# Layers 2 to 5 of a six-layer recurrent net: whole halves of the batch, weights stationary, gates turned in place of products

## The chip, the cores and the metric

One core of one Trainium2 chip. The metric is the device time of one execution in microseconds, as the median of several executions. TensorE (PE in the profile) multiplies, VectorE (DVE), ScalarE (ACT) and GpSimd (POOL) do the elementwise work, and transfers are issued from SyncE (SP), ACT and POOL. SBUF is the working memory, PSUM the memory that TensorE writes.

## The reference

```python
for i in range(6):                       # NLAYERS
    gate = ih[i][token]                  # (1024, 256), rows of a table of 4000
    state = jnp.tanh(state + jnp.matmul(state, hh[i]) * gate)
return state                             # (1024, 256) float32
```

Tokens run from 49 to 31985, the table has 4000 rows, and an index beyond its end takes the last row, number 3999. So about seven tokens in eight take that row.

## The kernel before, in words

The state is kept turned: 256 hidden units on partitions, as two blocks c = 0, 1 of 128, and the batch along the free dimension. The batch of 1024 is cut into four quarters of 256, each of two tiles of 128. A step n is a layer and a quarter (l, q = divmod(n, 4)); there are 24. All tensors of a step have 128 x 512 elements.

Layers 0 and 1 (`plain`, L353): state tiles are the stationary operand (128 x 128), the weights w[:, l, c, :] of 256 columns move, in plain float32, 8 matmuls a step. The product comes out with the batch on partitions, as the gates lie. DVE multiplies it with the gates (`gating`, L306, L312), TensorE turns it back with four transposes (`turn`, L396, L392), DVE adds the state (`sum_up`, L314, L317), ACT takes the tanh (`tanh`, L266, L271).

Layers 2 to 5 take rounded operands (type fp32r) in three parts. ACT writes the tanh a second time as rounded `sh` (L270), POOL writes what is lost as `sl = s - sh` (`low_state`, L230, L233), and the weights are split likewise (`round_weights` on ACT, L264; `low_weights` on POOL, L237). `high` (L366, L375) multiplies sh by the high and the low weights, 8 matmuls; `low` (L379, L384) multiplies sl by the high weights, 4 matmuls, into the same PSUM bank. `product` is both. TensorE runs product(n), then turn(n - 1) (L436 to L438). The last step is cut into its two tiles, so that the end of the chain runs on 256 elements (L440 to L453, and L340 to L349 on DVE, L280 to L284 on ACT); two last stores of one tile each follow (L193).

The gates: only rows below 3999 are fetched. Before it, the last row, spread over all partitions by TensorE transposes of a broadcast (L414) into the PSUM banks `spread`, is copied into `gate` by DVE and ACT (`fill`, L300 and L260; `DVE_FILLS`, `ACT_FILLS` give piece, first tile, tiles). POOL then fetches tile by tile with an indirect DMA that skips rows beyond the bound (`gather`, L221, L224), each after the fills of its tile. Tiles 0 and 1 are first fetched for layers 0 to 2 with all 128 rows (`gather_plain`, L207), and their second half of the columns is filled and fetched last (`gather_second_half`, L213).

Each engine runs its own list in the order written, and semaphores order them against each other. SP loads the four state quarters and the weights one behind the other, each waiting for the transfer two before it (L168 to L183). ACT runs the fills, then tanh(n) in order, with one layer's weights rounded behind tanh(0), (4), (8) and (12) (`ROUND_BEHIND`).

Of the kernel before, what the change touches and what calls it, by code (L numbers as in the profile page):

```python
# [4 lines left out]
P = 128  # L5
BATCH = 1024
# [5 lines left out]
LAST_QUARTER = QUARTERS - 1  # L12
# [6 lines left out]
STEPS = LAYERS * QUARTERS  # L19
LAST_LAYER = STEPS - QUARTERS  # L20
# [11 lines left out]
HALF = LAYERS // 2 * HIDDEN  # L32
FIRST_HALF, SECOND_HALF = slice(0, HALF), slice(HALF, 2 * HALF)
PLAIN_TILES = [0, 1]
# [4 lines left out]
PIECES = [(0, 2), (3, 2), (2, 1), (5, 1)]  # L39
# [7 lines left out]
FIRST_SPLIT = 2 * QUARTERS  # L47
LOW_STATE = list(range(FIRST_SPLIT - QUARTERS, LAST_LAYER))


LOW_WEIGHTS_BEHIND = {5: 3, 9: 4, 13: 5}


ROUND_BEHIND = {0: 2, 4: 3, 8: 4, 12: 5}


def recurrent_cells(nc, state_t, token, gate_rows, hh, out_t):
# [5 lines left out]
    half_table = table.rearrange("v (h n) -> (v h) n", n=HALF)  # L63
# [3 lines left out]
    out_v = out_t.rearrange("(c p) (q b) -> q p c b", p=P, q=QUARTERS)  # L67
    out_tile = out_t.rearrange("(c p) (t b) -> t p c b", p=P, t=TILES)
    w_v = hh.rearrange("l (c p) n -> l p c n", p=P)

    with ExitStack() as ctx:
# [6 lines left out]
        def quarter_sems(name):  # L78
            return [sem(f"{name}{q}") for q in range(QUARTERS)]

        tok = sb("tok", [P, TILES], i32)
# [4 lines left out]
        half_of = sb("half_of", [P, TILES], i32)  # L86
# [5 lines left out]
        s = sb("s", [P, QUARTERS, KC, QB], f32)  # L92
        sh = sb("sh", [P, QUARTERS, KC, QB], f32r)
        sl = sb("sl", [P, QUARTERS, KC, QB], f32r)
        pre = sb("pre", [P, QUARTERS, KC, QB], f32)
# [3 lines left out]
        prod = [ctx.enter_context(nc.psum_tensor(f"prod{q}", [P, TPQ, HIDDEN], f32)) for q in range(QUARTERS)]  # L99
        turned = [ctx.enter_context(nc.psum_tensor(f"turned{q}", [P, KC, QB], f32)) for q in range(QUARTERS)]  # L100


        spread = [bank.rearrange("p c b -> p (c b)")[:, 0:count * HIDDEN]
                  for bank, (_, count) in zip([turned[1], turned[2], turned[3], prod[3]], PIECES)]


        last_prod = [prod[LAST_QUARTER], prod[0]]
        last_turned = [turned[LAST_QUARTER], turned[0]]

# [9 lines left out]
        halves_ready = sem("halves_ready")  # L119
        rows_ready = sem("rows_ready")  # L120
        plain_in = [sem(f"plain_in{t}") for t in PLAIN_TILES]
# [13 lines left out]

        end_prod = sem("end_prod")
        end_gated = sem("end_gated")
        end_turn = sem("end_turn")
        end_pre = sem("end_pre")
        end_s = sem("end_s")  # L140
# [5 lines left out]

        def fills_of(t, fills):

            return max(i + 1 for i, (_, first, count) in enumerate(fills) if first <= t < first + count)

        def filled(i, t, count):
            first, layers = PIECES[i]
            return gate[:, t:t + count, first * HIDDEN:(first + layers) * HIDDEN]

        def filling(i, count):
            return spread[i].unsqueeze(1).to_broadcast([P, count, PIECES[i][1] * HIDDEN])

        with nc.Block() as block:

            @block.sync  # L160
            def _(sp):
                def load_state(q):
                    sp.dma_start(s[:, q], state_v[q]).then_inc(state_in[q], 16)
# [14 lines left out]
                load_weights(1)  # L178
                sp.wait_ge(state_in[3], 16)
                load_weights(2)  # L180
                for l in range(3, LAYERS):
                    sp.wait_ge(w_in[l - 2], 16)
                    load_weights(l)  # L183

                for q in range(QUARTERS - 1):
                    sp.wait_ge(s_ready[q], LAYERS)
                    sp.dma_start(out_v[q], s[:, q]).then_inc(out_done, 16)
                for t in range(TPQ):
                    if t == 0:
                        sp.wait_ge(s_ready[LAST_QUARTER], LAYERS)  # L190
                    else:
                        sp.wait_ge(end_s, t)
                    sp.dma_start(out_tile[LAST_QUARTER * TPQ + t],  # L193
                                 s[:, LAST_QUARTER, :, t * P:(t + 1) * P]).then_inc(out_done, 16)
                sp.wait_ge(out_done, 16 * (QUARTERS - 1 + TPQ))

            @block.gpsimd
            def _(pool):

                last_fetched = nc.gpsimd.to_reg(VOCAB - 2)  # L200
                last_half_fetched = nc.gpsimd.to_reg(2 * (VOCAB - 2))
# [5 lines left out]
                def gather_plain(t):  # L207
                    nc.gpsimd.indirect_dma_start(  # L208
                        gate[:, t, FIRST_HALF], None, half_table,
                        bass.IndirectOffsetOnAxis(half_of[:, t:t + 1].bitcast(u32), 0),  # L210
                    ).then_inc(plain_in[t], 16)

                def gather_second_half(t):  # L213
                    pool.wait_ge(filled_act, fills_of(t, ACT_FILLS))
                    nc.gpsimd.indirect_dma_start(
                        gate[:, t, SECOND_HALF], None, half_table,
                        bass.IndirectOffsetOnAxis(half_of[:, t:t + 1].bitcast(u32), 0),
                        element_offset=HALF, bounds_check=last_half_fetched, oob_is_err=False,
                    ).then_inc(gate_in[t], 16)

                def gather(t):  # L221
                    pool.wait_ge(filled_dve, fills_of(t, DVE_FILLS))
                    pool.wait_ge(filled_act, fills_of(t, ACT_FILLS))
# [6 lines left out]
                def low_state(n):  # L230
                    q = n % QUARTERS
                    pool.wait_ge(s_ready[q], done(n))
                    nc.gpsimd.tensor_tensor(sl[:, q], s[:, q], sh[:, q].bitcast(f32), ALU.subtract).then_inc(sl_ready[q], 1)  # L233
# [5 lines left out]
                pool.wait_ge(halves_ready, 1)  # L239
                for t in PLAIN_TILES:  # L240
                    gather_plain(t)
                pool.wait_ge(rows_ready, 1)
                for t in range(len(PLAIN_TILES), TILES):
                    gather(t)
                for t in PLAIN_TILES:
                    gather_second_half(t)
                low_weights(2)
                for n in LOW_STATE:
                    low_state(n)
                    if n in LOW_WEIGHTS_BEHIND:  # L250
                        low_weights(LOW_WEIGHTS_BEHIND[n])

            @block.scalar
            def _(act):
# [11 lines left out]
                def tanh(n):  # L266
                    q = n % QUARTERS
                    act.wait_ge(pre_ready[q], done(n))
                    if FIRST_SPLIT - QUARTERS <= n < LAST_LAYER:
# [207 lines left out]
```

## Time and profile before

| | us |
|---|---|
| median of 3 runs | 61.64 |
| lowest, highest | 61.51, 62.06 |
| the profiled execution | 61.56 |
| its span in the profile | 59.7 |
| PE busy in the span | 52.7 (88%) |
| POOL, DVE, ACT busy | 36.3, 37.2, 32.8 |

The span runs from the first to the last recorded instruction; the execution's time also holds what lies around it. Busy times of PE are of pipelined instructions, whose records overlap. The granted TensorE clock is 1.0 (full) over the whole span.

### The profile page before, as it was taken

Reading aid. Unit: us, or ns where it says so; the run is one execution under the profiler, and the core shown is the slowest. Engines: PE = TensorE matmul, PEld = TensorE weight load, DVE = VectorE, ACT = ScalarE, POOL = GpSimd, SP = SyncE. Lnnn points to the kernel's source line nnn. Section 1 sums busy time; section 2 is a strip of 40 time slices with the busy share of each in tenths; the row PEclk is TensorE's granted clock in tenths of the full one; section 3 lists DMA queues with packets and bytes.
Section 4 is the critical chain, followed back from the end, with each engine's and each line's share of the span. In section 5 each row is a group of like instructions: output and inputs, shape, how many; then the busy total and the mean of one; then the engine's idle time right before and its main releaser. Section 6 shows DMA issues by size and latency. Waiting matters only on the chain.

```text
span 59.7 us, 992 instructions
## 1 busy us (share of the span) xinstructions
PE 52.7 (88%) x369; PEld 49.1 (82%) x369; DVE 37.2 (62%) x61; ACT 32.8 (55%) x55; POOL 36.3 (61%) x36
## 2 busy tenths in 40 slices
PE   0899937998999999999999999999999999999600
PEld 0699806877889889899989999999999999999300
DVE  0236960598637867858746786667866688669810
ACT  0704999501272243994696557685576556744630
POOL 4076077716779300489998699786997866670000
PEclk9999999999999999999999999999999999999999
DMA  0686697893878600000000000000000000005384
GB/s 0 76 266 111 188 391 268 139 305 106 260 208 220 175 12 0 0 0 11 0 0 0 0 0 0 11 0 0 5 0 0 0 0 0 11 0 176 120 277 131
DMA packets 6196, 5.17 MB, mean 87 GB/s; under 512 B 2107, under 2 KB 5947, under 8 KB 6192
## 3 DMA queue, kind: packets, MB, share of 16 engines
q1 hardware_dynamic: 3952, 3.41, 18.7%
q0 software_dynamic: 1184, 1.43, 9.3%
q10 hardware_dynamic: 1056, 0.27, 2.0%
q8 instruction: 3, 0.05, 0.3%
q14 instruction: 1, 0.01, 0.0%
HBM read 8.92 MB, written 1.05 MB: 167 GB/s over the span
## 4 chain that ended last, share of the span: by engine, by line
PE 58%; DMA 21%; POOL 6%; ACT 5%; DVE 3%; issue 1%; SPq 1%
DMA s<-state_t_dram 21%; PE prod L375 21%; PE turned L392 14%; PE prod L362 12%; PE prod L384 12%; POOL sl L233 4%; POOL wr L237 2%; ACT sh L270 2%; ACT s L271 2%; DVE pre L317 1%; ACT wr L264 1%; DVE gp L345 1%; DVE pre L349 1%; ACT s L284 1%; SPq L168 1%
## 5 line engine op out<-in xcount | busy, mean ns | idle before, releaser
L233 POOL TENSOR_TENSOR sl<-s,sh 128x512 fp32r<-128x512 f32 x16 | 20.6, 1300 | 9.2 <-ACT s L271 9.2
L312 DVE TENSOR_TENSOR gp<-prod,gate 128x512 f32<-128x512 f32 x23 | 15.8, 689 | 12.6 <-PE prod L384 9.1
L375 PE MATMUL prod<-wr,sh 128*128 128x256 f32 x128 | 19.4, 293 | 0.0
L271 ACT ACTIVATE s<-pre 128x512 f32<-128x512 f32 x23 | 14.3, 620 | 8.5 <-DVE pre L317 8.5
L317 DVE TENSOR_TENSOR pre<-turned,s 128x512 f32<-128x512 f32 x23 | 15.7, 683 | 2.8 <-PE turned L392 2.8
L362 PE MATMUL prod<-w,s 128*128 128x256 f32 x64 | 15.5, 388 | 1.7 <-DMA s<-state_t_dram 1.7
L375 PEld LDWEIGHTS prod<-wr,sh 128*128 128x128 f32 x128 | 16.3, 190 | 0.0
L270 ACT ACTIVATE sh<-pre 128x512 fp32r<-128x512 f32 x16 | 10.1, 632 | 10.2 <-DVE pre L317 10.2
L362 PEld LDWEIGHTS prod<-w,s 128*128 128x128 f32 x64 | 12.0, 197 | 3.6 <-issue 2.3
L392 PE MATMUL turned<-ident,gp 128*128 128x128 f32 x96 | 14.5, 273 | 0.3 <-DVE gp L345 0.3
L392 PEld LDWEIGHTS turned<-ident,gp 128*128 128x128 f32 x96 | 11.3, 140 | 1.1 <-DVE gp L345 0.5
L384 PE MATMUL prod<-wr,sl 128*128 128x256 f32 x64 | 10.6, 285 | 0.1
L384 PEld LDWEIGHTS prod<-wr,sl 128*128 128x128 f32 x64 | 8.8, 191 | 0.3 <-POOL sl L233 0.3
L224 POOL DMA_INDIRECT gate<-gates_dram,row_of x6 | 6.0, 993 | 4.3 <-ACT gate L260 1.9
L300 DVE COPY gate<-turned 128x512 f32<-128x512 f32 (+1 forms) x7 | 5.5, 835 | 1.5 <-PE turned L414 1.5
L260 ACT COPY gate<-turned 128x1024 f32<-128x1024 f32 (+1 forms) x5 | 4.2, 869 | 2.0 <-PE turned L414 2.0
L237 POOL TENSOR_TENSOR wr<-w,wr 128x512 fp32r<-128x512 f32 x4 | 5.2, 1296 | 0.0
L208 POOL DMA_INDIRECT gate<-gates_dram,half_of x2 | 2.1, 1034 | 2.1 <-DVE half_of L294 1.8
L264 ACT CAST wr<-w 128x512 fp32r<-128x512 f32 x4 | 2.4, 606 | 1.4 <-DMA w<-hh_dram 1.4
L408 PE MATMUL turned<-ident 128*128 128x128 f32 x5 | 1.3, 432 | 1.6 <-POOL ident L204 1.6
L260 ACT COPY gate<-prod 128x512 f32<-128x512 f32 x4 | 2.5, 628 | 0.3 <-PE prod L414 0.3
L414 PE MATMUL turned<-ident,last_row 128*128 128x128 f32 x10 | 2.4, 426 | 0.1
(22 smaller groups left out, 11.4 us busy)
## 6 DMA issues: line engine op xcount, KB each, us to landing
w<-hh_dram SPq DMA_DIRECT2D x5, 256.0 KB, 3.6
s<-state_t_dram SPq DMA_DIRECT2D x4, 256.0 KB, 4.5
out_t_dram<-s SPq DMA_DIRECT2D x3, 256.0 KB, 2.2
w<-hh_dram ACTq DMA_DIRECT2D x1, 256.0 KB, 4.0
out_t_dram<-s SPq DMA_DIRECT2D x2, 128.0 KB, 2.0
gate<-gates_dram,row_of POOLq DMA_INDIRECT x6, 4.1
gate<-gates_dram,half_of POOLq DMA_INDIRECT x4, 4.5
last_row<-gates_dram ACTq DMA_DIRECT2D x1, 6.0 KB, 2.3
```

The source lines that it names most:

```text
L224: nc.gpsimd.indirect_dma_start(gate[:, t], None, table, bass.IndirectOffsetOnAxis(row_of[:, t:t + 1].bitcast(u32), 0), bounds_check=last_f ...
L233: nc.gpsimd.tensor_tensor(sl[:, q], s[:, q], sh[:, q].bitcast(f32), ALU.subtract).then_inc(sl_ready[q], 1)
L237: nc.gpsimd.tensor_tensor(wr[:, l, :, 1], w[:, l], wr[:, l, :, 0].bitcast(f32), ALU.subtract).then_inc(wl_ready, 1)
L260: nc.scalar.copy(filled(i, t, count), filling(i, count)).then_inc(filled_act, 1)
L270: nc.scalar.activation(sh[:, q], pre[:, q], ACT.Tanh).then_inc(sh_ready[q], 1)
L271: nc.scalar.activation(s[:, q], pre[:, q], ACT.Tanh).then_inc(s_ready[q], 1)
L312: nc.vector.tensor_tensor(gp[:, q], prod[q][:, :, :], gates_of(n, 0, TPQ), ALU.mult).then_inc(gated[q], 1)
L317: nc.vector.tensor_tensor(pre[:, q], turned[q][:, :, :], s[:, q], ALU.add).then_inc(pre_ready[q], 1)
L362: last = nc.tensor.matmul(prod[q][:, t, :], s[:, q, c, t * P:(t + 1) * P], w[:, l, c, :], start=c == 0, stop=c == KC - 1)
L375: nc.tensor.matmul(banks[t][:, t, :], sh[:, q, c, t * P:(t + 1) * P], wr[:, l, c, half], start=half == 0 and c == 0 and t == tiles[0], sto ...
L384: last = nc.tensor.matmul(banks[t][:, t, :], sl[:, q, c, t * P:(t + 1) * P], wr[:, l, c, 0], start=False, stop=c == KC - 1, skip_group_che ...
L392: last = nc.tensor.transpose(banks[t][:, c, t * P:(t + 1) * P], gp[:, q, t, c * P:(c + 1) * P], ident[:, :])
```

## The change

Layers 0 and 1 stay by quarters. For layers 2 to 5:

- The batch is cut into two halves h of 512, and a unit u = (h, c) is one half and one block c of 128 output hidden units, again 128 x 512. The weights are the stationary operand, wr[:, l, k, half, c*128:(c+1)*128], and the state's 512 columns move. So the product comes out turned already, with hidden units on partitions.
- In a half step TensorE runs the high products of both units (4 matmuls each), then for each unit its low ones (2) and 4 transposes of raw gates of the next half step (`turn_gates`).
- ACT copies the turned gates from PSUM to `gate_t` (`copy_gates`), ahead of each tanh. DVE multiplies product and gates in place in PSUM (`wide_gating`) and adds the state (`wide_sum`). ACT writes sh and s per unit, POOL sl per unit. sh and sl have two buffers, by layer.
- The last step is no longer cut; four stores of one unit each (256 KB) replace three of a quarter and two of a tile.
- Weights of layers 2 to 5 are rounded behind tanh(0), (1) and (2, two of them), and POOL splits all of them behind the gathers.
- The state loads 1 to 3 and the weight loads are each issued one transfer earlier on SP.
- Tiles 0 and 1 are fetched once, with the bound and without a fill ahead of it; DVE then writes the last row where a token is 3999 (`patch`, a predicated copy from the spread bank, by `is_last`). The spread row stands in three PSUM banks by pairs of layers (`PIECE` = 2), and DVE_FILLS and ACT_FILLS follow that. TensorE's turn(2) and turn(3) wait for the patches that read the same banks.

```diff
+WIDE = 2
+STEPS = WIDE * QUARTERS
+UNITS = HALVES * KC
-PLAIN_TILES = [0, 1]
+LATE_TILES = [0, 1]
-DVE_FILLS = [(0, 2, 1), (2, 2, 2), (0, 3, 1), (0, 4, 2), (2, 4, 2), (0, 6, 2), (2, 6, 2)]
-ACT_FILLS = [(1, 2, 1), (3, 2, 2), (1, 3, 1), (1, 4, 2), (3, 4, 2), (1, 6, 2), (3, 6, 2), (1, 0, 2), (3, 0, 2)]
+DVE_FILLS = [(0, 2, 1), (0, 3, 1), (0, 4, 2), (0, 6, 2)]
+ACT_FILLS = [(1, 2, 1), (2, 2, 1), (1, 3, 1), (2, 3, 1), (1, 4, 2), (2, 4, 2), (1, 6, 2), (2, 6, 2)]
-ROUND_BEHIND = {0: 2, 4: 3, 8: 4, 12: 5}
+ROUND_BEHIND = {0: [2], 1: [3], 2: [4, 5]}
...
 # SP
                 load_state(0)
+                load_state(1)
 
                 sp.wait_ge(state_in[0], 16)
-                load_state(1)
+                load_state(2)
                 sp.wait_ge(w_in[0], 16)
-                load_state(2)
+                load_state(3)
                 sp.wait_ge(state_in[1], 16)
-                load_state(3)
+                load_weights(1)
...
+                for h in range(HALVES):
+                    for c in range(KC):
+                        sp.wait_ge(unit_s[h * KC + c], wide_done(LAYERS - 1))
+                        sp.dma_start(out_v[h, c], of_unit(s, h, c)).then_inc(out_done, 16)
...
 # POOL
+                for t in range(TILES):
+                    gather(t)
+                for l in range(2, LAYERS):
+                    low_weights(l)
+                for q in range(QUARTERS):
+                    low_state(q)
+                for l in range(WIDE, LAYERS - 1):
+                    for h in range(HALVES):
+                        for c in range(KC):
+                            wide_low_state(l, h, c)
...
 # ACT
+                copy_gates(WIDE, 0, 0)
+                copy_gates(WIDE, 0, 1)
+                tanh(STEPS - 1)
+                for l in range(WIDE, LAYERS):
+                    for h in range(HALVES):
+                        l_next, h_next = (l, 1) if h == 0 else (l + 1, 0)
+                        for c in range(KC):
+                            if l_next < LAYERS:
+                                copy_gates(l_next, h_next, c)
+                            wide_tanh(l, h, c)
...
 # DVE
+                def patch(i, t, count):
+                    for late in range(t, t + count):
+                        dve.wait_ge(gate_in[late], 16)
+                    nc.vector.copy_predicated(filled(i, t, count),
+                                              is_last[:, t:t + count].unsqueeze(2).to_broadcast([P, count, PIECE * HIDDEN]),
+                                              filling(i, count)).then_inc(patched, 1)
...
+                def wide_gating(l, h, c):
+                    u = h * KC + c
+                    dve.wait_ge(unit_prod[u], wide_done(l))
+                    dve.wait_ge(gates_copied[u], wide_done(l))
+                    nc.vector.tensor_tensor(prod_bank[u][:, :], prod_bank[u][:, :], gate_t[:, u], ALU.mult).then_inc(unit_gated[u], 1)
+
+                def wide_sum(l, h, c):
+                    u = h * KC + c
+                    dve.wait_ge(unit_gated[u], wide_done(l))
+                    nc.vector.tensor_tensor(of_unit(pre, h, c), prod_bank[u][:, :], of_unit(s, h, c), ALU.add).then_inc(unit_pre[u], 1)
...
+                for i, t, count in DVE_FILLS[:3]:
                     fill(i, t, count)
+                dve.wait_ge(index_step, 3)
+                patch(0, 0, 1)
+                for i, t, count in DVE_FILLS[3:]:
+                    fill(i, t, count)
+                patch(0, 1, 1)
                 gating(0)
-                for i, t, count in DVE_FILLS[5:]:
-                    fill(i, t, count)
                 gating(1)
                 sum_up(0)
+                dve.wait_ge(filled_act, len(ACT_FILLS))
+                patch(1, 0, 2)
                 gating(2)
                 sum_up(1)
                 sum_up(2)
+                patch(2, 0, 2)
                 gating(3)
...
+                gating(7)
+                sum_up(6)
+                sum_up(7)
+                for l in range(WIDE, LAYERS):
+                    for h in range(HALVES):
+                        for c in range(KC):
+                            wide_gating(l, h, c)
+                            wide_sum(l, h, c)
...
 # TensorE
+                def wide_high(l, h, c):
...
+                    for half in range(2):
+                        for k in range(KC):
+                            nc.tensor.matmul(prod_bank[u][:, :], wr[:, l, k, half, c * P:(c + 1) * P],
+                                             of_unit(sh[:, (l - 1) % 2], h, k),
+                                             start=half == 0 and k == 0, stop=False, skip_group_check=True)
+
+                def wide_low(l, h, c):
...
+                    for k in range(KC):
+                        if l > WIDE:
+                            pe.wait_ge(unit_sl[h * KC + k], wide_done(l - 1))
+                        last = nc.tensor.matmul(prod_bank[u][:, :], wr[:, l, k, 0, c * P:(c + 1) * P],
+                                                of_unit(sl[:, (l - 1) % 2], h, k),
+                                                start=False, stop=k == KC - 1, skip_group_check=True)
+                    last.then_inc(unit_prod[u], 1)
...
                 turn(6)
-                for n in range(FIRST_SPLIT, STEPS - 1):
-                    product(n)
-                    turn(n - 1)
...
+                turn_gates(WIDE, 0, 0)
+                turn_gates(WIDE, 0, 1)
+                turn(7)
+                for l in range(WIDE, LAYERS):
+                    for h in range(HALVES):
+                        l_next, h_next = (l, 1) if h == 0 else (l + 1, 0)
+                        for c in range(KC):
+                            wide_high(l, h, c)
+                        for c in range(KC):
+                            wide_low(l, h, c)
+                            if l_next < LAYERS:
+                                turn_gates(l_next, h_next, c)
```

In the diff, `# SP` and the like are set in to say whose list a part belongs to.

## Rows read from the trace of the kernel before

**Rows 1.** Busy time by stage: from:to, length, each engine, clock, DMA share, GB/s.

```profile
30.00:55.54 25.54, 25.49 (x218) 25.46 (x218) 17.73 (x28) 16.09 (x28) 19.12 (x15) 1.00 0.04 12
55.54:59.70 4.16, 0.65 (x4) 0.20 (x2) 1.18 (x4) 1.46 (x3) 0.00 (x0) 1.00 0.58 189
```

**Rows 2.** The chain that ended last, in order of time: start, length, what.

```profile
9.27 4.34 DMA s<-state_t_dram
...
16.15 1.73 PE prod L362 x8
...
33.09 0.96 PE prod L375 x8
34.04 0.48 PE prod L384 x4
34.52 0.44 PE turned L392 x4
```

**Rows 3.** One line's instructions (ns, min/median/max), then groups (busy us, mean ns).

```profile
L375 PEld LDWEIGHTS prod<-wr,sh x128: 187/190/193, 25.0 to 54.9; 128*128 128x128 f32 x128
L375 PE MATMUL prod<-wr,sh x128: 277/283/365, 25.0 to 55.0; 128*128 128x256 f32 x128
...
L362 PEld LDWEIGHTS prod<-w,s 128*128 128x128 f32 x64 | 12.0, 197 | 3.6 <-issue 2.3
L392 PE MATMUL turned<-ident,gp 128*128 128x128 f32 x96 | 14.5, 273 | 0.3 <-DVE gp L345 0.3
L392 PEld LDWEIGHTS turned<-ident,gp 128*128 128x128 f32 x96 | 11.3, 140 | 1.1 <-DVE gp L345 0.5
```

**Rows 4.** Timeline, spacing of operations on ACT, DVE and POOL: start, length, engine.

```profile
5.91 0.59 ACT L260 COPY gate<-prod 128x512 f32<-128x512 f32 x1 [0.27 <-PE prod L414]
6.39 1.51 ACT L260 COPY gate<-turned 128x512 f32<-128x512 f32 x2
...
23.41 0.63 ACT L270 ACTIVATE sh<-pre 128x512 fp32r<-128x512 f32 x1 [1.54 <-DVE pre L317]
23.94 0.61 ACT L271 ACTIVATE s<-pre 128x512 f32<-128x512 f32 x1
...
28.64 0.69 DVE L312 TENSOR_TENSOR gp<-prod,gate 128x512 f32<-128x512 f32 x1 [0.59 <-PE prod L384]
28.70 3.82 POOL L233 TENSOR_TENSOR sl<-s,sh 128x512 fp32r<-128x512 f32 x3
...
29.25 0.68 DVE L317 TENSOR_TENSOR pre<-turned,s 128x512 f32<-128x512 f32 x1
```

**Rows 5.** The head: the timeline, then the gates' transfers from issue to landing.

```profile
5.67 2.26 PE L362 MATMUL prod<-w,s 128*128 128x256 f32 x8
...
8.25 1.05 ACT L260 COPY gate<-turned 128x1024 f32<-128x1024 f32 x1
...
9.93 0.99 POOL L224 DMA_INDIRECT gate<-gates_dram,row_of  x1 [0.30 <-ACT gate L260]
...
11.22 0.99 POOL L224 DMA_INDIRECT gate<-gates_dram,row_of  x1 [0.30 <-issue]
...
15.32 0.69 DVE L312 TENSOR_TENSOR gp<-prod,gate 128x512 f32<-128x512 f32 x1 [0.65 <-DMA gate<-gates_dram,row_of]
...
19.88 0.60 PE L392 MATMUL turned<-ident,gp 128*128 128x128 f32 x4
...
24.64 0.60 PE L392 MATMUL turned<-ident,gp 128*128 128x128 f32 x4
...
DMA to landing us min/median/max: 3.6/4.1/6.1
```

**Rows 6.** The end: the timeline, then the stores of a quarter.

```profile
55.13 0.40 PE L384 MATMUL prod<-wr,sl 128*128 128x256 f32 x2
...
56.98 0.42 ACT L284 ACTIVATE s<-pre 128x256 f32<-128x256 f32 x1 [0.21 <-DVE pre L349]
...
out_t_dram<-s SPq DMA_DIRECT2D x3, 256.0 KB, 2.2
```

More of the change, by code:

```diff
@@ L79, in quarter_sems, with unit_sems @@
             return [sem(f"{name}{q}") for q in range(QUARTERS)]
+        def unit_sems(name):
+            return [sem(f"{name}{u}") for u in range(UNITS)]
         tok = sb("tok", [P, TILES], i32)
@@ L118, in recurrent_cells @@
         index_step = sem("index_step")
[L119 removed]
         rows_ready = sem("rows_ready")
[L121 removed]
+        patched = sem("patched")
         filled_dve = sem("filled_dve")
@@ L151, in filled @@
         def filled(i, t, count):
-            first, layers = PIECES[i]
-            return gate[:, t:t + count, first * HIDDEN:(first + layers) * HIDDEN]
+            return gate[:, t:t + count, i * PIECE * HIDDEN:(i + 1) * PIECE * HIDDEN]
         def filling(i, count):
-            return spread[i].unsqueeze(1).to_broadcast([P, count, PIECES[i][1] * HIDDEN])
+            return spread[i].unsqueeze(1).to_broadcast([P, count, PIECE * HIDDEN])
         with nc.Block() as block:
@@ L398, in turn @@
                     pe.wait_ge(gated[q], done(n))
-                    turns(n, range(TPQ), [turned[q]] * TPQ, turn_ready[q])
-                def product(n):
-                    q = n % QUARTERS
-                    high(n, range(TPQ), [prod[q]] * TPQ)
-                    low(n, range(TPQ), [prod[q]] * TPQ, prod_ready[q])
+                    for t in range(TPQ):
+                        for c in range(KC):
+                            last = nc.tensor.transpose(turned[q][:, c, t * P:(t + 1) * P],
+                                                       gp[:, q, t, c * P:(c + 1) * P], ident[:, :])
@@ new lines, in turn, with turn_gates @@
+                    last.then_inc(turn_ready[q], 1)
+                def turn_gates(l, h, c):
+                    u = h * KC + c
+                    pe.wait_ge(gated[2 * h], 1)
+                    pe.wait_ge(gated[2 * h + 1], 1)
+                    if h == 0:
+                        pe.wait_ge(patched, l // PIECE + len(LATE_TILES))
+                    if l == WIDE:
+                        pe.wait_ge(pre_ready[u], WIDE)
+                    else:
+                        pe.wait_ge(gates_copied[u], wide_done(l - 1))
+                    for t in range(TPH):
+                        column = l * HIDDEN + c * P
+                        last = nc.tensor.transpose(turned_bank[u][:, t * P:(t + 1) * P],
+                                                   gate[:, h * TPH + t, column:column + P], ident[:, :])
+                    last.then_inc(gates_turned[u], 1)
@@ L409, in _ @@
                 pe.wait_ge(row_in, 16)
-                for i, (first, layers) in enumerate(PIECES):
-                    columns = spread[i].rearrange("p (l m c) -> p l c m", l=layers, m=P)
-                    for l in range(layers):
+                for i in range(PIECES):
+                    columns = spread[i].rearrange("p (l m c) -> p l c m", l=PIECE, m=P)
+                    for l in range(PIECE):
                         for c in range(KC):
-                            last = nc.tensor.transpose(columns[:, l, c], last_row[:, first + l, c:c + 1].to_broadcast([P, P]),
+                            last = nc.tensor.transpose(columns[:, l, c], last_row[:, i * PIECE + l, c:c + 1].to_broadcast([P, P]),
                                                        ident[:, :])
@@ L435, in _ @@
                 turn(6)
[L436 to L453 removed]
+                turn_gates(WIDE, 0, 0)
[6 more added lines that the diff above has]
+                            wide_high(l, h, c)
+                        for c in range(KC):
+                            wide_low(l, h, c)
+                            if l_next < LAYERS:
+                                turn_gates(l_next, h_next, c)
 def kernel(r_state, r_token, L0_rec_ih, L0_rec_hh):
```

237 lines of the change are left out of this document (92 added, 145 removed).

## The prediction, made before the changed kernel was run

> **What bounds the kernel now.** I read the windows by stage first, because one share for the whole run hides which engine sets each stage. From 30.00 to 55.54 us TensorE is busy 25.49 of 25.54 us, its weight loads 25.46, while DVE has 17.73, ACT 16.09 and POOL 19.12 [rows 1]. The granted clock stands at 1.00, the upper level, in both stretches. So through the layers in question only TensorE time counts. The reader then takes the chain of waits, which in that stretch is nothing but a repeating piece: 0.96 us for eight high products, 0.48 for four low ones, 0.44 for four transposes [rows 2], once per quarter step (16 times), 1.88 us each. Per instruction: 0.119 us for a 256-column product of rounded operands, 0.110 us for a transpose; and a plain float32 product of layers 0 and 1 (1.73 us for eight) takes 0.216 us for the same 256 columns. Before 13.7 us the chain is the fourth state load, landing at 13.61. The profiled execution took 61.56 us with a span of 59.7, so 1.86 us lie around the span; it stands 0.08 under the median of 61.64.
>
> **Part 1: the products of layers 2 to 5.** Before: 16 quarter steps x 12 = 192 products of 256 columns, 192 x 0.119 = 22.8 us. After: 16 units (4 layers x 2 halves x 2 column blocks) x 6 = 96 products of 512 columns. The trace has no rounded product of 512 columns. Lower bound: half of the present two, if weights cost nothing more, and nothing in the trace excludes that a column streams as fast as in a transpose or faster, 96 x 0.19 = 18.2. Upper bound: 2 x 0.119 = 0.238 each, 22.8, no saving. I take 0.216, which is what the nearest row shows for an instruction that streams 256 columns twice (the plain product), with a weight load of 197 ns beside it, about that of the rounded products (190) [rows 3]. The reason to put the present 0.119 on the weights and not on the columns: weight loads of the rounded products last 190 ns, those of the transposes 140, and the weight-load row is saturated (25.46 of 25.54), so each product now waits for its load; with twice the stream per load it is hidden. 96 x 0.216 = 20.7, a saving of 2.1 us. By the Trainium skill, "TensorE: Matmul & The Clock Gate", section "Back-to-back issue gap", the gap is N/2.4 ns plus 2.5, which is 216 ns at 512 columns but 109 at 256, where the row has 119; so this page and the trace differ at 256 and it cannot say where the other 10 ns come from. If they grew with the columns, the sum would be the upper bound.
>
> **Part 2: transposes.** Before, gated products are turned, 4 per quarter step; after, raw gates, 4 per unit, also 16 x 4 = 64. Cost unchanged (64 x 0.11 = 7.0 us), but they leave the path product, gating, turning, sum, and 8 of them stand before layer 2 and none in the last half step.
>
> **Part 3: does another engine take over?** A half step on TensorE is now 8 x 0.216 + 4 x 0.216 + 8 x 0.11 = 1.73 + 0.86 + 0.88 = 3.47 us. Against that, per half step (two units):
> DVE: gating 0.69, then the sum, which now waits for its own gating; the sum's next neighbour may start 0.61 after it (28.64 to 29.25) [rows 4]. 2 x (0.69 + 0.03 + 0.61) = 2.66. The gating now writes PSUM, which the trace does not show; between 0.6 and 1.0 us each it stays below 3.47. I take 0.69, the row of the same shape.
> ACT: a gate copy, a rounded and a plain tanh for each unit. By start-to-start times 0.48 (5.91 to 6.39), 0.53 (23.41 to 23.94) and 0.53 [rows 4]: 2 x 1.54 = 3.08. By their full durations (0.59 to 0.63) it would be 2 x 1.86 = 3.7, above 3.47. In a busy queue the rows show the first.
> POOL: 2 x 1.27 = 2.55 (three in 3.82) [rows 4].
> Then the loop of one half, with its step starting on TensorE at 0: low products of unit 0 are visible at 2.16 + 0.2 = 2.36, gating and sum to 3.78; unit 1 to 5.1; ACT rounds unit 1 by 5.75 and finishes its plain tanh by 6.3, POOL its low part by 7.6. The same half's next high products start at 6.94 (slack 1.2) and its low ones at 8.67 (slack 1.1). That the high products of both units stand first is what gives the 1.73 us of cover for POOL. The gate copy for the next unit is queued ahead of a tanh and waits for transposes ending at 2.8; ACT is idle then. So TensorE stays the bound and I cost these waits at nothing.
>
> **Part 4: the head.** State loads 1 to 3 are issued one step earlier, so the fourth no longer ends at 13.61. The two full-table gathers of 128 rows go; tiles 0 and 1 now fetch only their valid rows, unfilled, and DVE patches the rest. What is late next is the chain of gathers. ACT's fills: 512-wide from 5.91 every 0.48, and tile 4's two 1024-wide ones (1.05 for the first of that width before, [rows 5]) end near 9.35; so the gather of tile 4 is issued at 9.4, that of tile 5 1.3 later (9.93 to 11.22 before) at 10.7 instead of 11.22, and at 4.1 us to landing it is in at 14.8. Before: 11.22 + 4.1 = 15.32, which is exactly where DVE stopped waiting [rows 5]. From there: gating(2) to 15.5, sum_up(1) to 16.1, tanh(1) to 16.75, plain(5) to 18.5. In parallel turn(2) at 15.8, sum_up(2) to 17.1, the 1024-wide patch, gating(3) to 19.0 (tile 7 landed by 17.4). A predicated copy is not in the trace: bounds 0.6 to 1.4 for 512 elements (a DVE copy, and twice it); I take the 0.69 of a same-sized DVE operation [rows 4] and 1.2 for 1024. Turn(3) then runs at 19.05 instead of 19.88; after it TensorE is continuous as before (19.88 to 24.64 = 4.76 for two plain steps and three turns), so turn(6) ends at 24.25 instead of 25.08. Gain 0.8 us. Of the 2 us that the earlier state loads would give (plain(1) right behind plain(0), which began at 5.67), the rest is lost in waits for gates. Rounding of weights 4 and 5 moves behind tanh(2) near 18 us; the weight loads behind the earlier state loads are in by then, and POOL, which splits them at 1.3 us each, is through by about 21. Turn(4) ends at 21.65; sum, rounded and plain tanh follow by 23.7, POOL splits quarters 0 and 1 by 26.3, and layer 2's first low products want them at 24.25 + 0.88 (gates) + 0.44 (turn(7)) + 1.73 (high) = 27.3. Slack 1.0, cost nothing; with the cover gone it would be the excess over that.
>
> **Part 5: the end.** Before, the last step was cut into two tiles: last product recorded to 55.53, last tanh to 57.40, 1.87 us, then 2.3 us to the span's end [rows 1, 6]. After, the last two units of 512 end 0.43 apart and DVE serves one after the other: from the first one's end 0.69 + 0.03 + 0.61 + 0.69 + 0.03 + 0.68 = 2.73, tanh 0.05 + 0.63, together 3.4, less 0.43 = 3.0 from the last product. Cost 1.1 us, and 0.2 for a last store of 256 KB (2.2 us to landing) rather than 128.
>
> **Sum.** Turn(6) ends 24.25, + turn(7) 0.44 + gate transposes 7.04 + products 20.7 = 52.4, recorded 0.2 longer: 52.6 (before 55.53). + 3.0 + 2.3 + 0.2 = 58.1 us of span, + 1.86 = 60.0 us against 61.56: -2.1 products, -0.8 head, +1.3 end.
>
> **Rivals.**
> A, columns: the 0.119 is a cost per column. 96 x 0.022 = 2.1 us comes back: 62.1. For it: the recorded product lasts 283 ns (median) and a transpose, whose neighbours follow at 0.110, 273; those 10 ns are the difference in spacing too [rows 3]. Against it: the weight loads in the same rows.
> B, the other side, ACT becomes the bound: if gate copy and tanh of different buffers don't overlap as in the head, ACT needs 2 x 1.86 = 3.72 us plus its waits per half step, + 0.3 x 8 = 2.4 us: 62.4, slower than before. It decides as soon as a half step's six ACT operations take over 3.47 us; then TensorE shows a gap ahead of each first high product. Against it: starts 0.53 apart in rows 4.
> C, the patches cost the head its gain: each stands in DVE's queue ahead of gatings, and if one takes 1.4 us (2.4 for the wide ones) gating(3) ends 1.2 later: 61.2. The Trainium skill, "SBUF - State Buffer", section "Who interferes with whom", has it that a DVE instruction with two SBUF inputs shuts out GpSimd reads; a patch reads its mask there and perhaps its destination. In this kernel that would hold a gather's issue by one patch: the one near 9.5 stands beside tile 4's gather, 0.7 us, giving 60.7. No row shows it.
> D, gathers land sooner with about 0.6 MB less to move (3.6 us, the shortest in rows 5): head gain 1.4, 59.4.
>
> **Chances.** Forecast (59.3 to 60.7, D within it) 0.60; A 0.13; B and other stalls in the loop 0.12; C 0.15. Range: from 58.9 (D with a product at 0.21) to 62.3 (A with a little lost). About 1% is what a measurement can tell from no change. Faster by over 1% (below 61.0): 0.60 + 0.08 of C = 0.68. Within: most of A and the rest of C, 0.16. Slower: B and the upper part of A, 0.16.
>
> **What would show it.** Products of 128x512: eight in 1.73 us of chain (A: 1.9). No TensorE idle between about 26 and 52 us (B: gaps before high products, ACT named). The last plain turn at about 24.2. A last DVE sum that starts 2.05 us after the first of the last two gatings. The forecast is wrong if the half step is not 3.47 us, or turn(6) stands at 25 or later.

## The result: 1.8% slower, and the profile after

| | before | changed |
|---|---|---|
| median, us | 61.85 (61.51 to 63.16) | 63.03 (62.75 to 63.71) |
| ratio, 95% interval | | 1.0175 [1.0123, 1.0227] |
| profiled execution, span | 61.56, 59.7 | 62.75, 60.9 |

The medians are over all executions (four of each); a ratio and its interval leave out those more than 1.5% above the fastest of their kernel. The forecast was 60.0 us. The same kernel measured once more beside the experiments gave 1.0131 [1.0086, 1.0175]. First the chain of the changed kernel: the head, one half step, the end (start, length, what).

```profile
0.73 2.82 DMA last_row<-gates_dram
...
18.44 1.32 DVE gate L321
19.77 0.58 DVE gp L338
20.34 0.14 issue
20.48 0.63 PE turned L409 x4
...
30.84 1.85 PE prod L443 x8
32.69 0.47 PE prod L455 x2
33.16 0.44 PE turned L427 x4
33.59 0.46 PE prod L455 x2
34.06 0.44 PE turned L427 x4
...
55.05 0.71 DVE prod L349
...
56.40 0.70 DVE prod L349
...
57.12 0.70 DVE pre L354
...
57.84 0.63 ACT s L282
```

Eight rounded products of 512 columns take 1.85 us, 0.231 each, where the forecast had 0.216. A half step is therefore 3.65 us and not 3.47. The first line is new: the chain of before started with state loads [rows 2], this one with the 6 KB of the last row. And the last of the four patches (L321, the one for layers 4 and 5) stands in the chain just ahead of gating(3). Now two windows of the changed kernel, columns as in [rows 1].

```profile
40.00:44.00 4.00, 4.00 (x23) 3.27 (x23) 2.69 (x4) 3.56 (x8) 2.94 (x3) 1.00 0.02 6
...
58.50:59.00 0.50, 0.00 (x0) 0.00 (x0) 0.00 (x0) 0.00 (x0) 0.00 (x0) 0.50 0.41 152
```

TensorE is never idle in the wide phase, with ACT at 3.56 of 4.00 us. Its weight loads fell from saturated [rows 1] to 3.27 of 4. The mean granted clock of this execution is 0.979, but the clock has no part in this execution's loss: it is 1.00 up to 58 us and falls to 0.50 only after that, when TensorE has no work left. Then the timeline of the head and the end, against [rows 5, 6].

```profile
3.60 2.82 PE L468 MATMUL turned<-ident,last_row 128*128 128x128 f32 x12 [0.68 <-DMA last_row<-gates_dram]
...
6.46 5.23 ACT L256 COPY gate<-turned 128x512 f32<-128x512 f32 x7 [0.27 <-PE turned L468]
...
7.83 0.99 POOL L214 DMA_INDIRECT gate<-gates_dram,row_of  x1 [1.87 <-ACT gate L256]
7.89 1.96 ACT L256 COPY gate<-turned 128x1024 f32<-128x1024 f32 x2
...
10.63 0.99 POOL L214 DMA_INDIRECT gate<-gates_dram,row_of  x1 [0.53 <-issue]
...
11.93 0.99 POOL L214 DMA_INDIRECT gate<-gates_dram,row_of  x1 [0.30 <-ACT gate L256]
...
15.39 1.97 PE L400 MATMUL prod<-w,s 128*128 128x256 f32 x8 [0.63 <-issue]
...
18.18 1.97 PE L400 MATMUL prod<-w,s 128*128 128x256 f32 x8 [0.38 <-ACT s L267]
...
20.48 0.63 PE L409 MATMUL turned<-ident,gp 128*128 128x128 f32 x4 [0.34 <-DVE gp L338]
...
25.28 0.60 PE L409 MATMUL turned<-ident,gp 128*128 128x128 f32 x4
...
54.39 1.08 PE L455 MATMUL prod<-sl,wr 128*128 128x512 f32 x4
```

(The line at 7.89 is the part of ACT's seven fills that belongs to tiles 4 and 5; it ends at 9.85.) The stages side by side, in us of the two profiled executions. Turn(6) is done 0.44 after its first record begins (24.64 and 25.28), as in the forecast:

| | before | changed | forecast |
|---|---|---|---|
| turn(6) done | 25.08 | 25.72 | 24.25 |
| from there to the last product's recorded end | 30.45 | 29.75 | 28.35 |
| from there to the end of the last tanh | 1.87 | 3.00 | 3.0 |
| from there to the end of the span | 2.3 | 2.4 | 2.5 |

So the wide phase gave 0.70 us, the head cost 0.64 and the end with its store nearly 1.3: 1.2 us of span in all. The forecast of the span (58.1) missed by 2.8 us: 1.5 in the head and 1.4 in the products, less 0.1 behind the last tanh.

### The profile page after: what moved, and what is told of

It is laid out like the page before. It is cut to its first block, busy times and chain, and to the rows that moved or that the text cites. A ratio compares the mean times of both kernels' runs of the same rounds, so it can differ in the third digit from the quotient of the medians.

```text
span 60.9 us, 853 instructions
## 1 busy us (share of the span) xinstructions
PE 51.9 (85%) x273; PEld 43.4 (71%) x273; DVE 39.9 (66%) x60; ACT 40.0 (66%) x69; POOL 34.4 (56%) x34
## 4 chain that ended last, share of the span: by engine, by line
PE 79%; DVE 7%; DMA 5%; issue 3%; ACT 1%; DVEq 0%
PE prod L443 24%; PE prod L400 21%; PE turned L427 11%; PE prod L455 11%; PE turned L409 6%; PE turned L468 5%; DMA last_row<-gates_dram 5%; DVE prod L349 2%; DVE gate L321 2%; DVE pre L354 1%; ACT s L282 1%; DVE gp L338 1%; DVEq L335 0%; DVEq L337 0%; DVE pre L343 0%
## 5 line engine op out<-in xcount | busy, mean ns | idle before, releaser
L443 PE MATMUL prod<-sh,wr 128*128 128x512 f32 x64 | 16.7, 403 | 0.0
L349 DVE TENSOR_TENSOR prod<-prod,gate_t 128x512 f32<-128x512 f32 x16 | 11.1, 695 | 7.8 <-PE prod L455 7.8
L443 PEld LDWEIGHTS prod<-sh,wr 128*128 128x128 f32 x64 | 11.4, 189 | 2.1
L354 DVE TENSOR_TENSOR pre<-prod,s 128x512 f32<-128x512 f32 x16 | 11.1, 692 | 0.5
L455 PE MATMUL prod<-sl,wr 128*128 128x512 f32 x32 | 10.4, 411 | 0.0
L427 PE MATMUL turned<-ident,gate 128*128 128x128 f32 x64 | 9.4, 272 | 0.0
L275 ACT COPY gate_t<-turned 128x512 f32<-128x512 f32 x16 | 9.1, 576 | 0.0
L338 DVE TENSOR_TENSOR gp<-prod,gate 128x512 f32<-128x512 f32 x8 | 5.4, 686 | 2.5 <-DMA gate<-gates_dram,row_of 1.8
L343 DVE TENSOR_TENSOR pre<-turned,s 128x512 f32<-128x512 f32 x8 | 5.5, 686 | 2.0 <-PE turned L409 2.0
L409 PE MATMUL turned<-ident,gp 128*128 128x128 f32 x32 | 4.7, 274 | 0.3 <-DVE gp L338 0.3
```

What stands on the lines that cost most here:

```text
L275: nc.scalar.copy(gate_t[:, u], turned_bank[u][:, :]).then_inc(gates_copied[u], 1)
L349: nc.vector.tensor_tensor(prod_bank[u][:, :], prod_bank[u][:, :], gate_t[:, u], ALU.mult).then_inc(unit_gated[u], 1)
L354: nc.vector.tensor_tensor(of_unit(pre, h, c), prod_bank[u][:, :], of_unit(s, h, c), ALU.add).then_inc(unit_pre[u], 1)
L409: last = nc.tensor.transpose(turned[q][:, c, t * P:(t + 1) * P], gp[:, q, t, c * P:(c + 1) * P], ident[:, :])
L427: last = nc.tensor.transpose(turned_bank[u][:, t * P:(t + 1) * P], gate[:, h * TPH + t, column:column + P], ident[:, :])
L443: nc.tensor.matmul(prod_bank[u][:, :], wr[:, l, k, half, c * P:(c + 1) * P], of_unit(sh[:, (l - 1) % 2], h, k), start=half == 0 and k == 0 ...
```

## The experiments

The times are ratios to the kernel before, run beside each on the same chip. To compare heads without the chance in the last row's landing, I use the time from the first spread transpose (the row has landed) to the first instruction behind turn(6); "head" below means that. It is 25.00 - 3.05 = 21.95 before and 25.71 - 3.60 = 22.11 in the changed kernel.

**e1_rates: what a rounded product costs.** Seven series behind the last real product, whose results nobody reads (two of them shown). One execution.

```diff
+                for i in range(16):
+                    nc.tensor.matmul(turned_bank[0][:, :], weights[:, i % 2, 0, 0:P], moving[:, i % 2, 0:512], start=True, stop=True, skip_group_check=True)
...
+                for i in range(16):
+                    nc.tensor.matmul(turned_bank[0][0:64, :], weights[:, i % 2, 0, 0:64], moving[:, i % 2, 0:512], start=True, stop=True, skip_group_check=True)
```

> After the last real product, with the other engines almost idle, TensorE runs seven series of rounded products into banks nobody reads (the results are left unused): weights of 128 columns against 512, 256 and 128 moving columns, the form of the kernel before (state stationary, 256 weight columns moving), weights of 64 columns against 512 and 256, and a plain float32 one of 512. Theory COLUMN: a rounded column costs 0.44 ns whatever stands beside it, so 512 columns stay at 0.231 us, 256 at 0.119 in all forms, with 64 weight columns too. Theory LOAD: the weight load slows the stream beside it; then 64 weight columns give 0.22 at 512 and 0.11 at 256. Theory CONTENTION: the other engines slow it; then 512 takes 0.216 in this quiet stretch with 128 weight columns too. 128 moving columns: COLUMN gives 0.063 unless the load binds; a load that binds shows as a floor, about 0.11.

The chain over that stretch. The lines are, in this order: 512, 256 and 128 moving columns, the old form with 256, 64 weight columns with 512 and with 256, plain float32 with 512.

```profile
55.85 3.63 PE turned L508 x16
59.48 1.91 PE turned L510 x16
61.40 1.74 PE turned L512 x16
63.13 1.96 PE turned L514 x16
65.10 3.67 PE turned L516 x16
68.77 1.82 PE turned L518 x16
70.59 6.87 PE turned L520 x16
```

Divided by 16: 0.227, 0.119, 0.109, 0.122, 0.229, 0.114 and 0.429 us. The 128-column series is a floor: halving the columns from 256 took off only 0.010 us, so something else than the columns sets the 0.109, and the weight load, the same in both, is the reading (not tested apart). So a pair of load and product can follow the last after 0.109. The 0.119 of the kernel before lies above that, and 512 columns take 0.227 and not 0.216, so my step falls. Halving the weight columns doesn't help at 512 (0.229), so LOAD falls there; at 256 it takes off 5 of the 10 ns above the floor, so a small part of the 0.119 may be the load's after all. CONTENTION explains 4 ns at most (0.231 in the kernel, 0.227 here, not 0.216). COLUMN holds in its numbers, except that the quiet 0.227 is below its 0.231 and 64 weight columns gave 0.114 and not 0.119. Whether the surplus sits on each column or on each instruction stays open. With 128 weight columns, 512 and 256 moving ones differ by 0.108 us, which is what 256 columns take at 2.4 GHz (0.107), so there it looks like a fixed 13 ns; with 64 weight columns they differ by 0.115.

The plain float32 series needs care: its loop has 8 matmuls, the trace 16 records. Each plain matmul is recorded as two instructions, so 0.429 us is one record and 0.86 one matmul of 512 columns. It is the same in layers 0 and 1: a step there has four matmuls in the kernel (two tiles, two blocks) and eight records, so the "8 matmuls a step" of the description, and the 0.216 that the prediction took as its nearest row, count records.

**e7_narrow: the wide product's worth in the kernel.** Each product of 512 as two of 256.

```diff
+                            for b in range(2):
+                                nc.tensor.matmul(prod_bank[u][:, b * QB:(b + 1) * QB], wr[:, l, k, half, c * P:(c + 1) * P],
+                                                 of_unit(sh[:, (l - 1) % 2], h, k)[:, b * QB:(b + 1) * QB],
```

> The changed kernel with each rounded product of 512 columns made as two of 256 with the same weights (192 instead of 96). Theory COLUMN (a rounded column costs 0.45 ns): two of 256 cost 0.238 against 0.231 measured at 512, so 96 x 0.007 = 0.7 us more, a half step of 3.73 instead of 3.65. My prediction's step (0.216 at 512, and 0.119 set by the weight load): 2 us more. This shows what the wider product is worth in the kernel itself.

Ratio 1.0303 [1.0224, 1.0382], so 0.8 to 1.1 us over the changed kernel's two measurements. The chain has the reason, sixteen high products and then four low ones:

```profile
28.01 1.91 PE prod L444 x16
29.93 0.48 PE prod L457 x4
```

0.119 each, the half step 3.75 instead of 3.65: 0.8 us in eight. COLUMN's 0.7 fits, my 2 us don't. In this kernel the wider product is worth about 0.8 us by the trace.

**e2_old_head: the head of before with the wide phase.** Load order, fills, full gathers and gatings as in the kernel before; layer 5's weights are split behind layer 1's states.

```diff
-ROUND_BEHIND = {0: [2], 1: [3], 2: [4, 5]}
+ROUND_BEHIND = {0: [2], 1: [3], 3: [4], 4: [5]}
-LATE_TILES = [0, 1]
+PLAIN_TILES = [0, 1]
+PIECES = [(0, 2), (3, 2), (2, 1), (5, 1)]
...
```

> The changed kernel with the head of the kernel before: its load order, its pieces and fills, the two full gathers, no patches. (Weights of layers 4 and 5 are rounded behind tanh(3) and tanh(4), since they land later, and POOL splits layer 5's behind the states of layer 1.) Theory HEAD: the new head costs 0.6 to 0.8 us, so the last plain turn ends near 25.1 instead of 25.9 and the time is 62.2 us, 0.8 under the changed kernel. Rival: the head is no worse by itself and the loss comes from where the wide phase takes over; then the time stays within 0.3 us of the changed kernel.

Median 62.85 us (62.01 to 63.63, 4 runs), too spread for a ratio: the time doesn't decide between HEAD and its rival. Its trace says two things. The last row landed late here too, with the old load order:

```profile
0.73 2.95 DMA last_row<-gates_dram
...
3.73 2.40 PE L475 MATMUL turned<-ident,last_row 128*128 128x128 f32 x10 [0.75 <-DMA last_row<-gates_dram]
...
25.37 1.04 PE L434 MATMUL turned<-ident,gate 128*128 128x128 f32 x8
```

And from that landing the head took 25.37 - 3.73 = 21.64 us, 0.5 less than in the changed kernel. One profile each doesn't settle it: e9, below, has the same head at 22.86.

**e3_row_first: is the row late because of the second state load?**

```diff
+                sp.wait_ge(row_in, 16)
                 load_state(1)
```

> One edit to the changed kernel: SP waits for the last row's transfer (6 KB) before it issues the second state load. Theory ROW: the second state load delayed the last row from 3.05 to 3.55 us and with it all fills, the gathers of tiles 2 to 7 and the gatings; the row is back at 3.05, the gather of tile 5 is issued near 11.4 instead of 11.9, and the time falls by 0.4 us. Rival: the chain is set by ACT's eight fills and the patches, and what is won at the row is lost at the second state load, which lands later than plain(1) wants it; no change within 0.2 us.

Ratio 1.0266 [1.0156, 1.0376], 0.6 to 0.8 us slower than the changed kernel, where ROW had 0.4 faster and its rival no change; both missed. The row was as late (2.86 us) with nothing of the second load under way, and e4 and e5, which load in the changed kernel's order, had it after 2.2, so ROW is refuted. Why it is slower was not followed up. Over all profiled kernels (twelve) the row took 2.2, 2.2, 2.3, 2.3, 2.7, 2.8, 2.9, 2.9, 2.9, 3.0, 3.2 and 3.3 us, in both load orders. What sets it is open; every fill starts behind it, so it moves the start of the fills by up to 1 us, and the profile of before had a quick one (2.3), the changed one a slow one (2.8).

**e4_end_by_unit: the order of the last half step.**

```diff
+                        if l_next == LAYERS:
+                            for c in range(KC):
+                                wide_high(l, h, c)
+                                wide_low(l, h, c)
+                            continue
```

> One edit to the changed kernel: in the last half step each unit's low products stand right behind its high ones, so the first unit is done 0.92 us earlier and DVE's work on it lies beside the second unit's products. Theory END: two units on DVE one behind the other cost the end 1.0 us; from the last product to the last tanh 2.4 us instead of 3.0 to 3.4, and the time falls by 0.9 us to 62.1. Rival: the low part of the state from POOL is late for the earlier low products, and half or more of it is lost in a TensorE gap before them.

Ratio 1.0053 [1.0009, 1.0097]: 0.5 to 0.75 us under the changed kernel, where END had 0.9. The timeline of its end:

```profile
53.58 0.70 DVE L349 TENSOR_TENSOR prod<-prod,gate_t 128x512 f32<-128x512 f32 x1
...
54.29 0.61 PE L455 MATMUL prod<-sl,wr 128*128 128x512 f32 x2
54.31 0.69 DVE L354 TENSOR_TENSOR pre<-prod,s 128x512 f32<-128x512 f32 x1
54.94 0.70 DVE L349 TENSOR_TENSOR prod<-prod,gate_t 128x512 f32<-128x512 f32 x1
...
56.40 0.63 ACT L282 ACTIVATE s<-pre 128x512 f32<-128x512 f32 x1 [0.73 <-DVE pre L354]
```

The first unit's gating runs beside the second's products, and from the last product (54.90) to the last tanh (57.03) it is 2.1 us instead of 3.0. END is shown, and the low products show no gap.

**e5_patches_early: the new wait in the head.**

```diff
+                dve.wait_ge(filled_act, len(ACT_FILLS))
+                patch(1, 0, 2)
+                sum_up(0)
                 gating(1)
-                sum_up(0)
-                dve.wait_ge(filled_act, len(ACT_FILLS))
-                patch(1, 0, 2)
+                patch(2, 0, 2)
                 gating(2)
                 sum_up(1)
                 sum_up(2)
-                patch(2, 0, 2)
```

> One edit to the changed kernel, on DVE alone: the patch of layers 2 and 3 moves ahead of gating(1) with sum_up(0) behind it, the patch of layers 4 and 5 ahead of gating(2), both into waits for gathers. Theory PATCH: the 1.3 us patch between sum_up(2) and gating(3) is the wait that holds turn(3); without it turn(3) runs 0.4 to 0.5 us earlier and so does all behind it: 0.4 us off the changed kernel. Rival GATHER: gating(3) would have to wait for tile 7's gather, issued near 14.5 and 4 us under way, and nothing is won.

Ratio 1.0031 [0.9993, 1.0069], 0.6 to 0.9 us under the changed kernel, more than its theory had. The chain of waits no longer holds a patch, and what is late next is tile 5's gather:

```profile
11.19 4.62 DMA gate<-gates_dram,row_of
...
15.92 0.69 DVE gp L338
16.61 0.61 DVE pre L343
...
17.25 0.64 ACT s L267
...
18.02 1.97 PE prod L399 x8
19.98 0.44 PE turned L408 x4
```

Turn(3) stands right behind plain(5), with no wait. In six of the seven profiles with late patches TensorE waited for gating(3) there, 0.17 to 0.71 us (0.34 in the changed kernel); in e5 and e8 it did not. That is PATCH's mechanism, and the times of e5 and the changed kernel, whose intervals don't touch, show that the new place pays. How much of it is this wait stays open, for the heads scatter by more. By the measure above they are 22.11, 21.92, 22.22, 22.32, 22.60, 22.62 and 22.83 us for the changed head (the changed kernel twice, e4, e1, e3, e6, e7; mean 22.37), 22.07 and 21.81 with early patches (e5, e8; mean 21.94), and 21.95, 21.64 and 22.86 for the old head (before, e2, e9). No profile shows the new head ahead of the old one.

**e6_end_pieces and e8_both: the end in four pieces, and both edits.** The last half step as four pieces of 256 columns, each with its own products, gating, sum, tanh and store.

```diff
+                            for c, b in END:
...
+                                for half in range(2):
+                                    for k in range(KC):
+                                        nc.tensor.matmul(end_bank(c, b), wr[:, l, k, half, c * P:(c + 1) * P],
+                                                         of_end(sh[:, (l - 1) % 2], k, b),
...
+                                last.then_inc(end_prod, 1)
```

> The changed kernel with its last half step cut into four pieces of 128 x 256, each with high and low products of its own, one behind the other, and stores of 128 KB. Theory END: the whole of the end's loss goes: from the last product to the last tanh 1.4 to 1.6 us (3.0 in the changed kernel, 2.1 by units), so the time is 1.3 to 1.5 us under the changed kernel, near 61.6. Rival: low products now wait for POOL's low part of the state, which takes back over half of it.

> Both edits, patches early and the end in four pieces. If both theories hold the gains add: 1.8 us under the changed kernel, about 61.2, which is 0.5 us under the kernel before, all of it from the wider products (0.6 us) and none from a shorter path. If the wide phase has a loss that I haven't named, it stays at or above the kernel before.

e6: 63.05 us (61.59 to 65.82, 4 runs), inconclusive; its trace has 1.96 us from the last product to the last tanh. e8: 61.86 us (61.08 to 62.15, 12 runs), ratio 0.9970 [0.9937, 1.0004], 1.0 to 1.3 us under the changed kernel, where 1.8 had been expected, and level with the one before. The end of e8:

```profile
52.47 0.19 PEld L536 LDWEIGHTS prod<-sl,wr 128*128 128x128 f32 x1 [0.22 <-POOL sl L247]
...
54.61 0.40 PE L536 MATMUL turned<-sl,wr 128*128 128x256 f32 x2
54.83 0.42 DVE L411 TENSOR_TENSOR prod<-prod,gate_t 128x256 f32<-128x256 f32 x1
...
55.28 0.42 DVE L413 TENSOR_TENSOR pre<-prod,s 128x256 f32<-128x256 f32 x1
55.62 0.42 DVE L411 TENSOR_TENSOR turned<-turned,gate_t 128x256 f32<-128x256 f32 x1
...
56.54 0.42 ACT L320 ACTIVATE s<-pre 128x256 f32<-128x256 f32 x1 [0.38 <-DVE pre L413]
```

From the last product (55.01) to the last tanh (56.96) it is 1.95 us, not the 1.4 to 1.6 expected: a piece costs DVE 0.80 us (54.83 to 55.62) and TensorE 0.72 (piece products start at 53.41 and 54.13), so DVE falls behind, and the earlier low products wait 0.22 us for POOL, which is not the half of the gain that the rival had. That is nearly the 1.87 of the kernel before. Its last product ends at 55.01 against 55.53.

**e9_old_head_pieces and e10_changed_again.** e9 is e2's head with e6's end, e10 the changed kernel unedited.

> The head of the kernel before (as in e2) with the end in four pieces (as in e6). If the new head is only worth what its patches' place costs, this stands level with e8 (patches early, end in pieces), 0.1 to 0.3 us below the kernel before. If the old head is the better one by itself, it is 0.3 us under e8. Measured from the first transpose of the last row (so that the row's landing drops out), the last plain turn should end after 21.8 us as in e2.

> The changed kernel itself, unedited, once more, for the spread of its head: the last row's landing differed by 1 us between kernels that load it alike. Expected: 1.5 to 2% above the kernel before, and a last plain turn 22.3 us after the first transpose of the last row, whatever that row's landing.

e9: 1.0013 [0.9974, 1.0051], level with e8 within the intervals, so the heads aren't told apart by time. Its trace missed the expectation of 21.8 us by a full microsecond, with TensorE idle for 1.26 us ahead of plain(5), from a cause that the profile doesn't name:

```profile
4.01 2.39 PE L502 MATMUL turned<-ident,last_row 128*128 128x128 f32 x10 [1.04 <-DMA last_row<-gates_dram]
...
19.87 1.97 PE L433 MATMUL prod<-w,s 128*128 128x256 f32 x8 [1.26 <-issue]
...
26.87 1.04 PE L461 MATMUL turned<-ident,gate 128*128 128x128 f32 x8
```

e10: 1.0131 [1.0086, 1.0175], a little under what I expected; its row took 2.7 us and its head 25.37 - 3.45 = 21.92.

## Why the prediction was wrong, by its own steps

**What bounds the kernel**: right in the main. The changed kernel has no TensorE idle time in the wide phase. The one before had a wait of 0.3 us, which the prediction missed because it read windows and chain from 30 us on:

```profile
30.05 0.53 PEld L384 LDWEIGHTS prod<-wr,sl 128*128 128x128 f32 x4 [0.27 <-POOL sl L233]
```


**Part 1 failed in size.** The step was "the present 0.119 is set by the weight load, so at 512 columns it is 0.216". Measured 0.231, and 0.227 with the other engines quiet, while a load and its product can go at 0.109. 96 x 0.015 = 1.4 us of the saving was never there: 22.2 us of products against 22.9 (16 times the chain's 0.955 and 0.48), so 0.7 saved and not 2.1. The whole wide phase shortened by 0.70 too, but that equality is luck. The wait for POOL (0.3) and some 0.1 of smaller gaps went; against them stands one more set of four transposes (0.44), for turn(7) and the 16 sets of gates make 17 before the last product, where there had been 16. The prediction's sum holds that set, its closing tally ("-2.1 products") names neither. Rival A was right in kind; the row it rested on, 283 ns against 273 for a transpose, was the one to believe: the same 10 ns stood in the spacing. I gave it 0.13 since I read saturated weight loads as a cause. But the record of a load lasts about 190 ns whether the products follow at 0.109 or 0.227 (e1) or 0.231 (changed kernel), so below 190 ns the row is full whatever sets the pace.

**Part 2 and Part 3: right.** Transposes 0.44 for four; DVE gating in PSUM 0.70, ACT's order, POOL: none stopped TensorE, and rival B did not happen. (The case that ACT's operations don't overlap was the one to fear: 2 x 1.86 = 3.7 is above the measured half step of 3.65 too.)

**Part 4 failed**: turn(6) done at 24.25 forecast and 25.72 measured, and already turn(3) stood at 20.48 instead of 19.05. Three steps. First, the row landed 0.55 us later than in the profile of before, which I had taken as fixed. Second, I had tile 4's gather issued right at the end of its fills, at 9.4. The fills ended at 9.85, and POOL began the gather 0.8 us behind them, at 10.63, as it had begun tile 2's at 7.83 behind a fill that begins at 6.46 and ends near 7.05. So tile 5's gather went out at 11.93 and not at 10.7; in e4 with an early row it was 11.25, and before 11.22: nothing won there. These two put plain(5) at 18.18, where the forecast has about 16.75, and by its end turn(3) was 1.1 us late. TensorE had also waited 0.63 us for tanh(0), which held turn(2) back to 17.20 (forecast 15.8), and 0.38 for tanh(1); the earlier states could not help there. Third, DVE's 1.32 us patch between sum_up(2) and gating(3). It was in my chain at 1.2, but I did not ask whether it could hold turn(3) longer than plain(5) did: it held it for the last 0.34 us, which e5 and e8 don't have. Rival C named the patches, at a price (1.4 us each for 512) that they don't have: 0.73 and 1.31 for 512 and 1024. Its other mechanism, a patch that holds a gather's issue, doesn't show either: tile 2's gather began at 7.83, in the middle of a patch (7.53 to 8.26), and no further behind its fill than tile 4's.

**Part 5: right.** 3.0 us from the last product to the last tanh, as worked out; e4 and e8 show that it was the cut of the last step that had kept it at 1.87. The last sum starts 2.07 us after the first of the last two gatings (2.05 forecast). I had priced it and still let a saving of 2.1 us outweigh it; at the true 0.7 it decides the sign alone.

**Sum**: -0.70 wide phase, +0.64 head, +1.13 end, +0.13 store: +1.2 us of span. Of the head's part 0.55 is the row's landing in these two executions; whether the change has a share in that landing is open. The result lies above the range (62.3), because what rival A stands for (1.4 us) and a late head (1.5) came together, and the prediction priced them one at a time.

## What to carry to other kernels

A wider instruction is worth only the part of its present spacing that isn't streaming: measure the floor (the same instruction with fewer columns) and, if you can, the wide form itself before crediting the saving to a hidden weight load. When the unit of work doubles, everything behind the last product doubles with it; cut the last step, or run its units one after the other, in the same change. A wait moved off one transfer lands on the next late one: follow the gathers from the fill that frees them, POOL's start included, and put work without a deadline into the waits that an engine already has.

## What the runs showed of the hardware that I had not expected

With 128 weight columns rounded products carry about 13 ns over their columns at a granted clock of 1.00, the 2.4 GHz level (0.119 and 0.227 us at 256 and 512 columns, which take 0.107 and 0.213). Plain float32 and the transposes of layers 0 and 1 carry about 2.5, if each record is taken to stream its columns twice: 0.429 us for 512 columns and 0.109 for 128. The Trainium skill, "TensorE: Matmul & The Clock Gate", section "Back-to-back issue gap", gives N/2.4 ns plus 2.5 as the gap of a single matmul: the trace agrees for the last two with N counted twice, and not for rounded operands.

The granted clock doesn't tell TensorE's pace at the start. The twelve transposes of the last row take 2.82 us, 0.235 each, at a granted clock of 1.00, and the transposes of the same shape behind gating 0.109. No run here varies this.

A predicated copy from PSUM costs what a plain DVE copy does plus 6 to 8%: 0.73 us for 128 x 512 (0.69), 1.31 for 128 x 1024 (1.21).

A transfer of 6 KB took 2.2 to 3.3 us to land over twelve profiled executions, and all fills hang on it. Several kernels with the wide phase also spread more from run to run (e4: 61.28 to 63.84 in 10 runs, e10: 62.35 to 65.52 in 6) than the kernel before (61.35 to 62.65 in 13), but the two with early patches don't (e5: 61.70 to 62.66 in 10, e8: 61.08 to 62.15 in 12); the cause is open.
